# Routing of chunks 0 to 23 inside the end of the attention part, and row numbers multiplied by GpSimd and ScalarE

## The reference, cut to what matters

```python
h = _layernorm(x, axis=-1) * (1 + cb) + sb
probs = softmax(h @ router_w.T)
topv, topi = top_k(probs, 2)
topv = topv / (topv.sum(axis=-1, keepdims=True) + 1e-09)
cw = (one_hot(topi, 8) * topv[..., None]).sum(axis=1)
y = gelu(h @ w1[e]) @ w2[e]            # for every expert e
x = x + gb * (cw * y).sum over e
```

## Time and profile before

| | |
|---|---|
| runs before | 784.28, 786.01, 787.66 us; median 786.01 |
| profiled execution, first to last instruction | 776.0 us |
| its own time from outside | not recorded apart; the median lies 10.0 us above the span |
| busy | PE 714.8 us (92%), DVE 628.2, ACT 571.2, POOL 518.5 |
| attention part ends, routing, first gather | about 337, 337 to 367, 367.1 us |

### The profile page before, as it was taken

The page is one execution under the profiler, slowest core; times in us unless marked ns, Lnnn a source line. Parts: engine busy times, 40 slices in busy tenths (PEclk is TensorE's granted clock), DMA queues, the critical chain, the costliest instruction groups (busy, mean ns, idle before and its releaser), DMA issues.

```text
span 776.0 us, 24871 instructions
## 1 busy us (share of the span) xinstructions
PE 714.8 (92%) x8105; PEld 549.7 (71%) x8105; DVE 628.2 (81%) x1494; ACT 571.2 (74%) x1108; POOL 518.5 (67%) x535
## 2 busy tenths in 40 slices
PE   8799999999999999845799999999999999999994
PEld 5467777777777776634677777777777777777772
DVE  4999999999999888778577777777777777777773
ACT  2799899999999998740476767777776767677772
POOL 5777777777777776547466666666666666666642
PEclk9999999999999999855799999999999999999997
DMA  6324344444443412310343343344333333443410
GB/s 226 113 67 133 110 135 120 131 120 139 124 140 116 151 64 67 120 48 8 96 77 69 71 73 74 76 70 79 70 75 69 77 69 76 76 72 76 72 21 1
DMA packets 52854, 69.27 MB, mean 89 GB/s; under 512 B 8864, under 2 KB 44080, under 8 KB 52736
## 3 DMA queue, kind: packets, MB, share of 16 engines
q0 software_dynamic: 18176, 27.06, 18.6%
q1 hardware_dynamic: 34560, 40.61, 16.9%
HBM read 46.50 MB, written 22.05 MB: 88 GB/s over the span
## 4 chain that ended last, share of the span: by engine, by line
PE 51%; DVE 2%; POOL 2%; issue 1%; DMA 1%; ACT 0%; POOLq 0%; DVEq 0%; ACTq 0%
PE hidden L1457 16%; PE bank L1475 15%; PE hidden L1459 8%; PE bank L1477 8%; PE bank L1292 2%; POOL mod_b L960 1%; PE bank L1309 0%; DMA xt<-ffn_rows,gi 0%; DMA out_dram<-x,si 0%; DVE stage L651 0%; PE bank L1300 0%; PE bank L1389 0%; POOL out_dram L1008 0%; DVE feat L652 0%; POOL mod_b L962 0%
## 5 line engine op out<-in xcount | busy, mean ns | idle before, releaser
L1457 PE MATMUL hidden<-qstT,w1hi_k 128*128 128x256 f16 x1136 | 197.9, 274 | 0.7 <-DVE qstT L755 0.7
L1459 PE MATMUL hidden<-qstT,w1lo_k 128*128 128x128 f16 x1136 | 193.6, 220 | 0.0
L1475 PE MATMUL bank<-w,amhi 128*128 x568 | 188.4, 379 | 0.1
L1477 PE MATMUL bank<-w,amlo 128*128 x568 | 154.8, 273 | 0.0
L1008 POOL DMA_INDIRECT out_dram<-x,si x71 | 115.2, 1622 | 38.8 <-issue 25.8
L791 DVE TENSOR_TENSOR amlo<-am,amhi 128x512 f16<-128x512 f32 x142 | 98.3, 693 | 49.2 <-ACT am L1168 49.2
L1457 PEld LDWEIGHTS hidden<-qstT,w1hi_k 128*128 x1136 | 111.7, 98 | 14.0 <-issue 1.1
L1459 PEld LDWEIGHTS hidden<-qstT,w1lo_k 128*128 x1136 | 111.6, 98 | 0.2
L1309 PE MATMUL bank<-wq,hT 128*128 128x512 f32 (+1 forms) x256 | 98.8, 511 | 1.3 <-DVE hT L524 1.2
L1475 PEld LDWEIGHTS bank<-w,amhi 128*128 128x128 f16 x568 | 55.6, 98 | 59.9 <-issue 0.4
L1167 ACT ACTIVATE amhi<-am 128x512 f16<-128x512 f32 x142 | 88.1, 620 | 0.3 <-DVE am L785 0.3
(11 more groups left out here) (219 smaller groups left out, 1783.6 us busy)
## 6 DMA issues: line engine op xcount, KB each, us to landing
stage<-in_L_ffn_w_dram SPq DMA_DIRECT2D x32, 512.0 KB, 4.3
xt<-in_L_attn_x_dram SPq DMA_DIRECT2D x32, 128.0 KB, 4.0
out_dram<-x SPq DMA_DIRECT2D x32, 128.0 KB, 3.7
ffn_rows<-h SPq DMA_DIRECT2D x32, 128.0 KB, 1.8
ffn_rows<-am SPq DMA_DIRECT2D x32, 128.0 KB, 4.2
am<-mod_rows SPq DMA_DIRECT2D x16, 128.0 KB, 4.0
mod_b<-mod_rows SPq DMA_DIRECT2D x8, 256.0 KB, 4.4
w<-in_L_wmod_dram SPq DMA_DIRECT2D x6, 256.0 KB, 4.6
```

The lines of the kernel that those rows point to most:

```text
L1457: t.matmul(dst.rearrange("p (q n) -> p q n", q=2), w1s[0][k][g][:, w_], both, start=(k == 0), stop=False)
L1459: last = t.matmul(dst[:, P:2 * P], w1s[1][k][g][:, w_], both[:, 0, :], start=False, stop=(k == KT - 1))
L1475: t.matmul(y[:, :], ghi[:, m.p, c_m], w2s[mt // 2][:, bass.ds(w_, 2 * D)], start=(mt == 0), stop=False)
L1477: last = t.matmul(y[:, D:2 * D], glo[:, m.p, c_m], w2s[mt // 2][:, bass.ds(w_, D)], start=False, stop=(mt == MT - 1))
```

## The change

It has six parts.

1. `SOON` is 24. The two largest logits, the sums, the ranks within an expert and the place tiles of group 0 of chunks 0 to 23 are made by entries in the closing tables (`m1`, `is1`, `oh1`, `m2`, `is2`, `oh2`, `picks`, `place`, `sums`, `ranks`, `tiles`). The place of a token within its block no longer depends on the experts' starts: an expert's start is a multiple of a block, so it is only added to the block number (`bases`, a tree of three additions).
2. Behind the tables VectorE makes the place tiles of groups 1 to 3, then routes chunks 24 to 31, makes group 4, waits for the ranks, and makes groups 5 to 7. All block tiles follow.
3. Row numbers are multiplied into the place tiles of groups 0 and 1 by GpSimd, of groups 2 to 4 by ScalarE, and into the block tiles of groups 5 to 7 by VectorE as before.
4. For chunks 28 to 31 `h2T` transposes the normalised row, and ScalarE puts scale and shift on in its copy (two instructions with a bias and a scale per partition). GpSimd still does `xm2` and `h2`, for the stored row, and `xm2` then waits for `h2T`.
5. Of the ranks of chunks 24 to 31 the sums of earlier chunks are added by eight matmuls with ones, without ScalarE between.
6. `e_row` is made by 6 GpSimd instructions in place of 12, one of them for 7 experts at once, and the shares by one instruction behind it, where they were ahead of it.

```diff
-SOON = 28
+SOON = 24
+PLACED_SOON = 2 * SOON // TG
+ID_POOL, ID_ACT = (0, 1), (2, 3, 4)
+TILE_ORDER = (0, 2, 3, 5, 6, 7, 1, 4)
+FOLDED = NC - CPB
...
@@ CLOSING_POOL
-    ("h2", 29), ("rs", 35), ("xm2", 30), ("h2", 30), ("rs", 36), ("xm2", 31), ("h2", 31), ("wb", 31))
+    ("xm2", 29), ("h2", 29), ("xm2", 30), ("h2", 30), ("rs", 36), ("id", 0), ("xm2", 31), ("shift", 0), ("h2", 31),
+    ("wb", 31))
...
@@ vector engine
+            def picks_soon(m):
+                dve.wait_ge(s_pe, PE_SOON)
+                rank_products(soon, 0)
+                run_and_place(soon)
...
+            def place_tiles(g):
+                v.tensor_tensor(places_of(g), places_by_tile, spread(in_place, g, P), ALU.is_equal)\
+                    .then_inc(b_["place"], 1)
...
+            for g_ in range(1, PLACED_SOON - 2):
+                place_tiles(g_)
             dve.wait_ge(a_["lge"], NC)
-            top_two(SOON, NC)
+            largest(rest)
+            marks["m1"] = link.n
...
+            for n_ in (4, 2, 1):
+                link(v.tensor_tensor(bases[:, :, 0:n_, :], bases[:, :, 0:n_, :], bases[:, :, n_:2 * n_, :], ALU.add))
+            link(v.tensor_tensor(by_list(in_block), bases[:, :, 0, :], by_list(in_run), ALU.add))
+
+            for g_ in range(PLACED_SOON - 1, 2 * NC // TG):
+                place_tiles(g_)
...
+            for k_, g_ in enumerate(TILE_ORDER):
+                block_tiles(g_)
+                if g_ not in ID_POOL + ID_ACT:
+                    dve.wait_ge(b_["block"], k_ + 1)
+                    v.tensor_tensor(group_of(blocks_in, g_, TB), group_of(blocks_in, g_, TB), spread(id_flat, g_, TB),
+                                    ALU.mult).then_inc(b_["tile"], 1)
@@ GpSimd
+                if part == 1 and m.n >= FOLDED:
+                    wait(pool, a_["h2T"], m.n + 1)
...
+            def place_ids(g_):
+
+                pool.wait_ge(b_["place"], g_ + 1)
+                g.tensor_tensor(ids_of(g_), places_of(g_).rearrange("p n t -> p t n"),
+                                id_flat[:, g_ * TG:(g_ + 1) * TG].rearrange("p (t u) -> p t u", u=1)
+                                .broadcast_to([P, TG, P]), ALU.mult).then_inc(b_["pool"], 1)
...
+            for g_ in ID_POOL[1:]:
+                place_ids(g_)
+
+            pool.wait_ge(s_dve, marks["nblk"])
+            ends = nblk_c[:, 0:E - 1].rearrange("p (e u) -> p e u", u=1).broadcast_to([P, E - 1, TB])
+            link(g.tensor_tensor(fits[:, 0:E - 1, :], blocks[:, :].rearrange("p (u j) -> p u j", u=1)
+                                 .broadcast_to([P, E - 1, TB]), ends, ALU.subtract))
+            link(g.tensor_scalar(fits[:, 0:E - 1, :], fits[:, 0:E - 1, :], 0.0, None, ALU.is_ge))
@@ ScalarE
+                for k in range(KT):
+                    last = v.activation(h2T[:, k * P:(k + 1) * P], h2_bank(m)[:, k * P:(k + 1) * P], ACT.Identity,
+                                        bias=mod_c[:, k:k + 1], scale=mod_c[:, KT + k:KT + k + 1])
...
+            def place_ids(g_):
+
+                act.wait_ge(b_["place"], g_ + 1)
+                for u in range(TG):
+                    i = (g_ * TG + u) // 2
+                    last = copy(ids_of(g_)[:, u, :], places_of(g_)[:, :, u], row_id[:, i:i + 1])
+                last.then_inc(b_["act"], 1)
@@ TensorE
+            t.matmul(local[:, :, SOON:NC], upto[:, :], chosen[:, :, SOON:NC], start=False, stop=True, skip_group_check=True)
+            for i in range(SOON, NC):
+                last = t.matmul(local[:, :, i + 1:NC + 1], ones[:, :], chosen[:, :, i:i + 1].broadcast_to([P, E, NC - i]),
+                                start=False, stop=True, skip_group_check=True)
...
+                for u in range(TG):
+                    rows = ids_of(g_)[:, u, :] if g_ in ID_POOL + ID_ACT else places_of(g_)[:, :, u]
+                    last = t.matmul(bank[7][:, 0:TB], rows, group_of(blocks_in, g_, TB)[:, :, u],
+                                    start=(k_ == u == 0), stop=(k_ == len(TILE_ORDER) - 1 and u == TG - 1))
```

More of the change, by code:

```diff
@@ L243, in adaln_block @@
         id16 = sb("id16", [P, NC, 2], F16)
[L244 to L246 removed]
+        rank = ra[:, 0:4 * NC].rearrange("p (u k i) -> p u k i", u=2, k=2)
+        in_block, in_place, in_run = (ra[:, (4 + u) * NC:(5 + u) * NC].bitcast(F16) for u in range(3))
+        bases = ra[:, 8 * NC:16 * NC].bitcast(F16).rearrange("p (k e i) -> p k e i", k=2, e=E)
         w_q = wq[:, :, :].rearrange("p k n -> p (k n)")
@@ L255, in adaln_block @@
         shares = w_q[:, 3 * D:3 * D + E * NC]
+        m1, m2, best = w_q[:, 624:656], w_q[:, 656:688], w_q[:, 688:704].bitcast(F16)
+        part, nblk, nblk_c, ones_e = (w_q[:, 704 + E * k:704 + E * (k + 1)] for k in range(4))
+        base = w_q[:, 736:736 + E // 2].bitcast(F16)
+        mod_c = sb("mod_c", [P, 2 * KT])
         gi = sb("gi", [P, GB, 2], U32)
@@ L336, in adaln_block @@
         s_modgb = sem("s_modgb")
+        s_modc = sem("s_modc")
         s_w = [sem("s_w0"), sem("s_w1")]
@@ L347, in adaln_block @@
         s_ms = sem("s_ms")
-        b_ = counters("b_", "block tile")
+        b_ = counters("b_", "place pool act block tile")
         c_ = counters("c_", "gi gs xh xl xT xTe hA hB lA lB sA sB gA gB glA glB y yl ys yw")
@@ L609, in weights_low, with over_e, each, largest @@
                 last.then_inc(a_["wlo"], 1)
+            def over_e(t):
+                return t.rearrange("p e i -> p i e")
+            lg = logits[:, :, :]
+            soon, rest = slice(0, SOON), slice(SOON, NC)
+            def each(r, c_):
+                return r[:, c_].rearrange("p (u i) -> p u i", u=1).broadcast_to([P, E, c_.stop - c_.start])
+            def largest(c_):
+                link(v.tensor_reduce(m1[:, c_], over_e(lg[:, :, c_]), AX_X, ALU.max))
+            def next_largest(c_):
+                link(v.scalar_tensor_tensor(out=masked[:, :, c_], in0=first[:, :, c_], scalar=OUT,
+                                            in1=lg[:, :, c_], op0=ALU.mult, op1=ALU.add))
+                link(v.tensor_reduce(m2[:, c_], over_e(masked[:, :, c_]), AX_X, ALU.max))
@@ new lines, in equal_to, with onehot, either @@
+            def equal_to(c_, vals, m_):
+                link(v.tensor_tensor(ranked[:, :, c_], vals[:, :, c_], each(m_, c_), ALU.is_equal))
+                link(v.tensor_tensor(ranked[:, :, c_], ranked[:, :, c_], rev[:, :, c_], ALU.mult))
+            def onehot(c_, oh):
+                link(v.tensor_reduce(best[:, c_], over_e(ranked[:, :, c_]), AX_X, ALU.max))
+                link(v.tensor_tensor(oh[:, :, c_], ranked[:, :, c_], each(best, c_), ALU.is_equal))
+            def either(c_):
+                link(v.tensor_tensor(chosen[:, :, c_], first[:, :, c_], second[:, :, c_], ALU.add))
@@ new lines, in largest_soon, with next_largest_soon, second_soon, by_list @@
+            def largest_soon(m):
+                wait(dve, a_["qk"], NC)
+                wait(dve, a_["v"], NC)
+                wait(dve, a_["lge"], SOON)
+                largest(soon)
+            def next_largest_soon(m):
+                next_largest(soon)
+            def second_soon(m):
+                onehot(soon, second)
+                link(v.memset(chosen[:, :, rest], 0.0))
+                either(soon)
+                marks["chosen_soon"] = link.n
+            def by_list(t):
+                return t.rearrange("p (i k) -> p k i", k=2)
@@ L1374, in h2_transpose @@
             def h2_transpose(m):
-                wait(pe, a_["h2"], m.n + 1)
+                wait(pe, a_["h2" if m.n < FOLDED else "xn2"], m.n + 1)
                 if m.n < NC - 3:
@@ L1391, in router, with chunk_sums, ranks_soon @@
                 last.then_inc(a_["lg"], 1)
+            def chunk_sums(m):
+                pe.wait_ge(s_dve, marks["chosen_soon"])
+                wait(pe, a_["sl1"], NC)
+                for half in range(2):
+                    last = t.matmul(bank[5][:, half * P:(half + 1) * P], chosen_flat[:, half * P:(half + 1) * P],
+                                    ones[:, :], start=True, stop=True)
+                last.then_inc(s_pe, 1)
+            def ranks_soon(m):
+                wait(pe, a_["stl"], (CPB - 1) * B)
+                t.matmul(local[:, :, 0:SOON], upto[:, :], chosen[:, :, 0:SOON], start=True, stop=False,
+                         skip_group_check=True)
+                pe.wait_ge(s_act, ACT_TOTAL)
+                for half in range(2):
+                    e_ = slice(half * E // 2, (half + 1) * E // 2)
+                    last = t.matmul(local[:, e_, :], totals[:, half, :], chunks_before[:, :, :], start=False, stop=True,
+                                    skip_group_check=True)
+                last.then_inc(s_pe, 1)
             works = {
@@ L1397, in _ @@
                 "aT": a_transpose, "pj": projection, "h2T": h2_transpose, "lg": router,
+                "sums": chunk_sums, "ranks": ranks_soon,
                 "mod1": second_modulation}
```

214 lines of the change are left out of this document (109 added, 105 removed), and 22 rows, old and new, of tables (CLOSING_ACT, CLOSING_DVE, CLOSING_PE, CLOSING_POOL).

## The result

The changed kernel took 791.08 us (median of 7 runs, 789.54 to 793.79), the kernel before in runs beside it 786.6 us (7 runs, 784.28 to 787.66): ratio 1.0066, 95% interval [1.0053, 1.008]. The forecast was 786.4 us with a range of 779.5 to 790.5. The change costs about 5 us; it was forecast at +0.4.

A forecast was written before the change was run, and what follows sets the result against it. It took the stretch before the first gather as the bound, on VectorE's and GpSimd's paths. The steps put the gather at 367.6 against 367.14 (+0.4): span 776.4 plus 10.0 makes 786.4 us (case A, chance 0.52), range 779.5 to 790.5.

The forecast's parts named there:

- Step 8: TensorE's tile matmuls: with contiguous weights 0.06 us apart, so the pass takes 6.2 us, 12.8 before.
- Step 1: Routing of chunks 0 to 23 in the closing: some 5.5 us of VectorE hidden in gaps, cost 0, up to 1 us.
- Step 2: Chunk 31 comes later: `x1` 31 at 335.3 (+1.2 us), `nb` 31 at 338.7 (+2.4).
- Step 3: Folded scale and shift take 2.1 us off the way from `xn2` to `h2T`; last logits at 342.1 (+0.4).
- Step 4: VectorE behind `nb`: two `wlo`, three place tiles, 2.25 us held by GpSimd's 2.4 us multiply; ready at 344.8.
- Step 5: Routing of the last eight chunks: 3.7 us with holds of 0.4 and 0.4, `chosen` at 348.5 (before 346.24).
- Step 6: Ranks about 1.0 us instead of 1.43, block numbers 3.5 plus 0.9 held; `in_block` done at 353.9.
- Step 7: GpSimd's second multiply holds VectorE 2.25 us, the 128x504 subtraction 1.1, small sums 0.5; first block tile at 360.0.
- Step 9: After the tile matmuls: `gi` 0.84 us behind, gather 0.3 behind that, at 367.6 (+0.4); ScalarE's groups 8.6 us, cost 0.
- The 10.0 us around the span: Added to the forecast span of 776.4 us, since the runs' median was 786.01 over a span of 776.0.
- Rival C: GpSimd's multiply is longer than 2.4 us, each us costing 2: 788.0 at 3.2, 791.2 if TensorE's pace stays 0.14; chance 0.18.
- Rival B: GpSimd's instructions hold VectorE little: gather at 358.9 (-8.2 us), 777.8 us, or 782 with half the holding; chance 0.30.

The follow-up runs named there:

- experiment 7: Base 2 plus 48 unused matmuls behind the last tile matmul, in four sets varying weights and moving operand: 0.129, 0.060, 0.027 and 0.060 us apart.
- experiment 9: Base 2 with added VectorE, GpSimd and ScalarE instructions at different access steps in idle time; GpSimd's 128x1024 multiply took 1.89 us contiguous, 2.31 at a 16-byte step.
- experiment 4: Changed kernel without GpSimd's multiplies, ranks of chunks 0 to 23 and place tile 0 moved behind the last `wlo`: ratio 1.003 to the kernel before.
- experiment 8: Base 2 with the fold undone, GpSimd again doing the last chunks' scale and shift ahead of the transpose: ratio 1.0047 to the kernel before.
- experiment 10: The kernel before with only the folded scale and shift for chunks 28 to 31 and the engine order that goes with it: ratio 1.0008.
- experiment 5: Base 2 with place tiles 5 to 7 made between the block tiles: ratio 0.9984 to the kernel before.
- Base 2: The kernel of experiment 2: the changed kernel without GpSimd's multiplies, ratio 1.0002 to the kernel before.
- experiment 2: Changed kernel without GpSimd's multiplies, VectorE multiplying groups 0 and 1 on the block tiles: ratio 1.0002 to the kernel before.
- experiment 1: Changed kernel with only GpSimd's first multiply of row numbers moved behind `xm2` of chunk 31: ratio 1.0049 to the kernel before.
- experiment 3: Changed kernel, GpSimd's multiplies kept, ranks of chunks 0 to 23 and place tile 0 moved behind the last `wlo`: ratio 1.0075 to the kernel before.
- experiment 6: The kernel of experiment 5 with GpSimd's subtraction and sums for the experts' numbers waiting for the first block tile: ratio 0.998 to the kernel before.

## Why the prediction was wrong

The forecast for the first gather was 367.6, the trace has 372.0 (its start-up taken off). Of the 4.4 us, 1.5 had been lost by `chosen`, 0.6 was won back up to the first block tile (10.9 us behind `chosen` instead of 11.5), 2.8 were lost from there to the last tile matmul, and 0.7 from there to the gather.

- **Step 8 failed, the largest term.** The sentence "with contiguous weights 72 columns at 1.2 GHz, 0.06, should be the pace" took the step of the weights for the cause of 0.14. The moving operand, the block tiles, kept its step. Measured: 0.130 for the multiplied groups, 0.135 for the others, 8.62 us for the pass instead of 6.2; experiment 7 shows the cause.
  The matmuls of the earlier trace rows, from which I took the hope, move 17 columns each. That row numbers multiplied in by ScalarE buy so little on TensorE follows from it. No version with contiguous block tiles was run. By experiment 9 such an order costs VectorE some 0.7 us a tile (1.17 and not 0.46), an estimate of 5.7 us for the eight, against some 4.5 on TensorE (64 times 0.07), so whether it would pay stays open.
- **Step 1 was wrong ("hidden, 0").** The ranks of the first 24 chunks took 3.0 us just ahead of `x1` 31. Of the 3.6 us by which `x1` 31 is late, 2.2 are theirs by experiment 4, 0.6 GpSimd's holds on them, and 0.7 came ahead of `xn2` 28. The gaps in which I placed them were partly filled by `wlo` 30, itself held to 1.82. Experiment 4 also shows that moving them does not help, since VectorE is then the bound.
- **Step 2:** `x1` 31 at 337.7 and not 335.3, for that reason. I had put 1.2 us down to TensorE; in the fourth experiment, with TensorE's new order, it comes 13.0 us behind `xn2` 28, before 12.9.
- **Step 3:** the fold works as forecast in kind; its worth depends on who waits (2.5 us in experiment 8, none in experiment 10).
- **Step 4 had the mechanism and the length right (2.31 us against 2.4) and the place wrong.** I let `nb` slip in ahead of the multiply. It came 0.07 us behind its start and was held for 2.1 us. That moved the last logits to 346.2; the `wlo` and three place tiles that I had counted in front of the routing then lay in the wait for them. That the result at `chosen` is off by only 1.5 is luck: it hides a wrong victim and `x1` 31 2.4 us later than forecast.
- **Step 5** was right within 0.1 (3.75 us from the start of the last chunks' routing to `chosen`, forecast 3.7). **Step 6** came out a little shorter (ranks back in 0.65 us, not 1.0).
- **Step 7** was right for the long instructions: the second multiply held the tree for 2.1 us, the 128x504 subtraction the next instruction for 0.8. Wrong was that the single-input comparison holds nothing: a place tile beside it took 1.11 us and not 0.68; in experiment 5 a block tile there took 0.73 instead of 0.46. Wrong too was the rule that VectorE's instructions with one SBUF input are not touched (line 691 above, the casts of experiment 9).
- **Step 9:** 0.3 from `gi` to the gather was too low; it was 0.94, of which 0.86 is issue. Base 2 has 0.85 there. GpSimd had stood at that wait for 5 us both times, which I had taken to shorten it. ScalarE's three groups took 10.2 us and not 8.6, which cost nothing: by the trace they ended at 358.2, and TensorE took the first of them at 364.3.
- **The 10.0 us around the span** were misread. The profiled execution of after took 791.15 us over a span of 789.3, 1.8 us more; the rest fits another chip (an expert part of 415.5 and not 408.9 us, 6.7) and a later start-up (1.7). This enters the sum on both sides and so does not change the difference.
- **Rival C's time (791.2) was nearly met, but not its cause:** the multiply was not longer; only its second condition, the pace that stays at 0.14, came true. Rival B is excluded by the 2.27 and 2.35 us above and by experiment 2. I had weighed the pace of 0.14 only together with a longer multiply; by itself it makes A 789.6, and it should have had a chance of its own.
- **Two small slips in the sums:** seven groups from 354.50 to 363.87 are 1.34 us each, not 1.39, and 341.9 + 2.25 + 0.5 is 344.65, not 344.8. Nothing hangs on either.

## What to carry to other kernels

An instruction moved to GpSimd is not free while VectorE is on the path: here each tensor-tensor of 2.3 us cost about its own length, and moving it only chose another victim (experiments 1 and 3). When a matmul's pace looks too slow, ask of both operands how they lie; here it was the moving one. And where one engine's tiles feed another engine, make them in the order in which they are used, not all of one kind first: experiments 5 and 6 are the only versions whose whole interval lies under the kernel before, by 0.2%, while taking the multiplies off GpSimd only brought the change back to even.

## What the runs showed of the hardware

- TensorE at the lower clock, 72 moving columns of 16-bit numbers: 0.060 us apart when contiguous, 0.129 at a step of 16 bytes, with contiguous weights in both (experiment 7). With the weights at such a step too, 0.135.
- VectorE's 128x576 multiply went from 0.46 to 3.22 us when each number was written 144 bytes behind the last; ScalarE's copy from 0.68 to 2.76 (experiment 9).
- A GpSimd tensor-tensor holds more of VectorE than I had: a cast of 5 numbers (1.38 us instead of 0.17, experiment 9) and a single-input TENSOR_SCALAR of 128x48 32-bit numbers (line 691: 0.41 us beside GpSimd's line 942, 0.19 without, in experiment 2). The reduction of line 688 kept its 1.08 us, but it had begun 0.76 us ahead of GpSimd's line, so whether a reduction that comes second is held stays open.
- The Trainium skill ("SBUF — State Buffer"), section "Who interferes with whom", names two kinds of VectorE instruction that GpSimd can block: those in a mode that uses the shared second pair of ports, and those with two SBUF inputs. `nb`, with its two inputs, agrees (2.27 us instead of 0.16). The casts and line 691 would be of the first kind; no run here shows in which mode they ran.
